# Expert stage of a graph and mixture network: 40 tiles of 384 tokens in place of 56 of 256, and down products with the weights stationary

## The reference, cut to what matters

```python
N_ROWS, D, E, H, TOP_K = 6250, 256, 8, 1024, 2
logits = xt @ Wr + br
top_p, top_idx = top_k(softmax(logits), TOP_K)
weights = top_p / top_p.sum(-1, keepdims=True)
xn = (xt - mean(xt)) * rsqrt(var(xt) + 1e-5)
xe = xn[None] * ln_g[:, None, :] + ln_b[:, None, :]
h = gelu(einsum('end,edh->enh', xe, W1) + b1[:, None, :])
y = einsum('enh,ehd->end', h, W2) + b2[:, None, :]
out = (weights[:, :, None] * y_of_the_two_chosen_experts).sum(1)
```

## Time and profile before

| | before |
|---|---|
| median of 3 runs | 7407.15 us (7395.56 to 7407.92) |
| the profiled execution's own time | 7444.26 us |
| its span, first to last instruction | 7442.4 us |
| mean granted TensorE clock | 0.717 |
| first expert transpose to last expert product | 4033.57 to 5615.09 us |
| POOL busy | 3724.7 us (50%) |
| PE busy | 3556.7 us (48%) |

### The profile page before, as it was taken

How to read it: one execution, slowest core, us unless ns; L and a number is a source line. 1 busy time by engine, 2 the same in 40 slices (tenths; PEclk the granted TensorE clock), 3 DMA queues, 4 the chain that set the end, 5 groups by cost and what they waited for, 6 DMA issues and landing times. The chain is left out here.

```text
span 7442.4 us, 64871 instructions
## 1 busy us (share of the span) xinstructions
PE 3556.7 (48%) x13693; PEld 2571.0 (35%) x13694; DVE 2821.2 (38%) x6837; ACT 831.5 (11%) x2066; POOL 3724.7 (50%) x3797
## 2 busy tenths in 40 slices
PE   3113964444433444444331222299991455555429
PEld 1001543333322333333230100178881334333317
DVE  5106854344435344344380000011114455555761
ACT  0001930000002000000130000022221100000222
POOL 4772046666662666666507766600005566666221
PEclk7556977777766777777655555599995777777759
DMA  3001023333311333332012000022214233333140
GB/s 133 1 0 37 12 59 91 92 91 90 92 41 50 90 90 91 90 92 84 1 40 92 2 4 4 9 73 79 82 56 137 86 90 90 89 90 89 56 159 18
DMA packets 290139, 497.46 MB, mean 67 GB/s; under 512 B 99253, under 2 KB 182880, under 8 KB 290048
## 3 DMA queue, kind: packets, MB, share of 16 engines
q0 software_dynamic: 163264, 345.19, 16.3%
q1 hardware_dynamic: 125696, 150.28, 6.2%
q10 hardware_dynamic: 1088, 1.05, 0.1%
HBM read 487.50 MB, written 92.89 MB: 78 GB/s over the span
## 5 line engine op out<-in xcount | busy, mean ns | idle before, releaser
L956 PE MATMUL sum_sums<-sum_got,sum_onehot 128*128 x4992 | 1583.0, 477 | 1780.9 <-DVE acc L1118 1392.7
L888 POOL DMA_INDIRECT sum_got<-xn,edge_row x1568 | 1534.1, 978 | 1175.3 <-issue 449.0
L956 PEld LDWEIGHTS sum_sums<-sum_got,sum_onehot 128*128 128x128 f32 x4992 | 1145.5, 239 | 2203.4 <-issue 2004.8
L1118 DVE TENSOR_TENSOR acc<-acc,sum_sums 128x257 f32 (+1 forms) x2496 | 1052.4, 422 | 1808.9 <-remote 1213.4
L888 POOL DMA_INDIRECT sum_got<-h,edge_row x784 | 754.0, 962 | 493.9 <-issue 223.9
L1248 POOL DMA_INDIRECT table<-rec,addr x784 | 762.4, 972 | 347.4 <-issue 305.5
L1754 PE MATMUL moe_f_ps_y<-xb,moe_f_hT 128*128 128x256 f32 x1792 | 475.8, 398 | 298.0 <-issue 297.8
L1738 PE MATMUL moe_f_ps_h<-moe_f_xT,xb 128*128 128x256 f32 x1792 | 472.1, 397 | 285.5 <-issue 285.5
L1819 DVE TENSOR_TENSOR moe_f_y<-moe_f_ps_y,moe_b 128x256 f32<-128x256 f32 x112 | 42.3, 419 | 1337.6 <-PE moe_f_ps_y L1754 650.6
L1248 POOL DMA_INDIRECT table<-sort_rec,sort_addr x392 | 404.5, 1032 | 199.3 <-issue 119.7
L1586 POOL DMA_INDIRECT moe_out_c_got<-moe_out,place_i x98 | 95.1, 971 | 815.5 <-PEq L1544 777.0
(11 more groups left out here) (481 smaller groups left out, 3420.1 us busy)
## 6 DMA issues: line engine op xcount, KB each, us to landing
xb<-in_L_ffn_W SPq DMA_DIRECT2D x112, 1024.0 KB
sum_got<-xn,edge_row POOLq DMA_INDIRECT x1568
moe_in<-acc SPq DMA_DIRECT2D x28, 512.0 KB
moe_f_xin<-moe_in SPq DMA_DIRECT2D x56, 256.0 KB
moe_out<-moe_f_y SPq DMA_DIRECT2D x56, 256.0 KB
xn<-xb SPq DMA_DIRECT2D x14, 896.0 KB
table<-rec,addr POOLq DMA_INDIRECT x784
sum_got<-h,edge_row POOLq DMA_INDIRECT x784
```

The costliest lines, as they stand in the source:

```text
L888: pool.indirect_dma_start(got[:, c % SU, 0:D], None, source, bass.IndirectOffsetOnAxis(ap=p.edge_row[:, c:c + 1], axis=0)).then_inc(s_got[ ...
L956: mm = nc.tensor.matmul(sums[k % 2][j], onehot[:, (k % QUARTERS) * HALF + j, :], flat(got[:, bass.ds(where[n % PLAN], 1), :]), start=True, ...
L1118: v.tensor_tensor(a, a, sums[k % 2][j], ALU.add).then_inc(s_added[j], 1)
```

## The change

The expert stage gets a function of its own, `moe`, with tiles of `MT` = 384 rows (`MC` = 3 blocks of 128) and `MOE_TILES` = 40. The up products move 384 columns. The down products have the 128 x 128 blocks of W2 stationary and move the 384 columns of `hT`; the result `yT` has D on partitions, so b2 becomes one number a partition (`p.moe_b2` is [128, 2, 8] and not [128, 8, 256]), the zero product goes, and the new `back` turns the result with 6 transposes, which VectorE copies to `y`. `flip` has 6 transposes. PSUM is dealt out anew: two banks `ps_f` shared by `flip` and `back`, four `ps_h`, two `ps_y`. On TensorE `flip(t+2)` now comes behind the first two ups of the tile, and `back(t-1)` behind the ups of j = 4 and 5. On SP the store of tile t-1 comes ahead of the weight loads. Four tiles are written out ahead of the loop in place of two. `Binning.starts` counts full tiles by comparing with multiples of 384. The zero fill of `moe_in` covers 15360 rows in place of 14336.

```diff
-MOE_TILES = (TOP * N + EX * (FT - 1)) // FT
+MC = 3
+MT = MC * P
+MOE_TILES = (TOP * N + EX * (MT - 1)) // MT
+MOST = -(-N // MT)
...
-        c.link(nc.vector.tensor_copy(self.total_i[:], self.total[:, 0:B + 1]))
-        c.link(nc.vector.tensor_single_scalar(self.total_i[:], self.total_i[:], shift, ALU.arith_shift_right))
-        c.link(nc.vector.tensor_copy(self.full[:], self.total_i[:]))
+        wide = [P, B + 1, MOST]
+        c.link(nc.vector.tensor_tensor(self.past[:], self.total[:, 0:B + 1].unsqueeze(2).to_broadcast(wide),
+                                       self.step[:].unsqueeze(1).to_broadcast(wide), ALU.is_gt))
+        c.link(nc.vector.tensor_reduce(self.full[:], self.past[:], AX, ALU.add))
...
+        ps_f = [p.ps(f"f_ps_f{i}", [P, 512], ctx) for i in range(2)]
+        ps_h = [p.ps(f"f_ps_h{i}", [P, 512], ctx) for i in range(4)]
+        ps_y = [p.ps(f"f_ps_y{i}", [P, 512], ctx) for i in range(KB)]
...
+            def store(t, k):
+                sp.wait_ge(s_y, 2 * t + 2)
+                sp.dma_start(at(y_dram, t), y[:, k, :, :]).then_inc(s_out[k], 16)
...
                 if left > 4:
-                    sp.wait_ge(s_flip, t + 3)
+                    sp.wait_ge(s_flip, KB * (t + 3))
                     load_x(t + 4, k)
+                if not (isinstance(t, int) and t == 0):
+                    store(t - 1, 1 - k)
+
                 gate(sp, s_down, t + 1, s_seen)
...
-                sp.wait_ge(s_y, 2 * t + 2)
-                sp.dma_start(at(y_dram, t), y[:, k, :, :]).then_inc(s_out[k], 16)
...
+                for kb in range(KB):
+                    if kb == 0:
+                        pe.wait_ge(s_x[k], 16 * uses + 16)
+                    if isinstance(t, int) and t in (1, 2, 3):
+                        pe.wait_ge(s_xT, KB * (t - 1) + kb + 1)
+                    elif not (isinstance(t, int) and t == 0):
+
+                        pe.wait_ge(s_y, 2 * t - 8 + kb + 1)
+                    for b in range(MC):
+                        last = nc.tensor.transpose(ps_f[kb][:, b * P:(b + 1) * P], xin[:, k, b, kb * P:(kb + 1) * P],
+                                                   p.ident[:])
+                    last.then_inc(s_flip, 1)
+
+            def back(t, left):
+
+                pe.wait_ge(s_yT, KB * t + KB)
+                for a in range(2):
+                    if left > 2:
+                        pe.wait_ge(s_xT, KB * (t + 3) + a + 1)
+                    else:
+                        pe.wait_ge(s_y, 2 * t - 2 + a + 1)
+                    for b in range(2 * a, min(2 * a + 2, MC)):
+                        for d in range(KB):
+                            last = nc.tensor.transpose(ps_f[a][:, (b % 2) * D + d * P:(b % 2) * D + (d + 1) * P],
+                                                       yT[:, d, b * P:(b + 1) * P], p.ident[:])
+                    last.then_inc(s_back, 1)
...
-                if j % 2 == 0 and not first:
-
-                    pe.wait_ge(s_act, HB * t - HB + j + 2)
+                if not (first and j < 4):
+
+                    pe.wait_ge(s_act, HB * t + j - 3)
...
-                    nc.tensor.matmul(ps_y[k][:].rearrange("p b d -> p (b d)"), zero[0:1, 0:P], zero, start=True, stop=False)
-                if j % 2 == 0:
-                    pe.wait_ge(s_act, HB * t + j + 2)
-                for blk in range(2):
-                    mm = nc.tensor.matmul(ps_y[k][:, blk, :], hT[:, k, j, blk * P:(blk + 1) * P], w2[:, wk, j, :],
-                                          start=False, stop=(j == HB - 1 and blk == 1))
+                    if not (isinstance(t, int) and t == 0):
+
+                        pe.wait_ge(s_yT, KB * t)
+                    pe.wait_ge(s_w2[k], 16 * uses + 16)
+                pe.wait_ge(s_act, HB * t + j + 1)
+                for d in range(KB):
+                    mm = nc.tensor.matmul(ps_y[d][:, 0:MT], w2[:, k, j, d * P:(d + 1) * P], hT[:, k, j, :],
+                                          start=(j == 0), stop=(j == HB - 1))
...
             def tile(t, k, uses, left):
-                if left > 2:
-                    flip(t + 2, k, uses + 1)
                 for j in range(0, HB, 2):
                     if left > 1:
                         for a in (j, j + 1):
                             up(t + 1, 1 - k, uses + (1 if k == 1 else 0), a)
+                    if j == 0 and left > 2:
+                        flip(t + 2, k, uses + 1)
+                    if j == 4 and not (isinstance(t, int) and t == 0):
+                        back(t - 1, left)
                     for a in (j, j + 1):
                         down(t, k, uses, a)
...
             def tile(t, k, uses, left):
                 if left > 2:
-                    evacuate(t + 2, k, uses + 1)
...
+                    enter(t + 2, k)
+                if not (isinstance(t, int) and t == 0):
+                    leave(t - 1, 1 - k, uses if k == 1 else uses - 1)
+                e = expert(dve, t)
                 dve.wait_ge(s_down, t + 1)
...
+                for d in range(KB):
+                    v.tensor_scalar(yT[:, d, :], ps_y[d][:, 0:MT], b2[:, d, bass.ds(e, 1)], None,
+                                    ALU.add).then_inc(s_yT, 1)
...
-                        (p.moe_b2[:, e, :], io["L0_ffn_b2"][e, :].partition_broadcast(P))]
+                        (p.moe_b2[:, :, e], columns(io["L0_ffn_b2"][e, :]))]
```

More of the change, by code:

```diff
@@ L1464, in _ @@
                 c.done(v.tensor_scalar(past[:], p.node_no[:], float(N), None, ALU.is_ge))
-                c.done(v.tensor_scalar(gap[:, 0:1], p.part_no[:], float(MOE_TILES * FT), None, ALU.add))
+                c.done(v.tensor_scalar(gap[:, 0:1], p.part_no[:], float(MOE_TILES * MT), None, ALU.add))
                 c.settle()
@@ L1594, in _, with moe @@
                 norm.apply_part(act, p.acc, p.xb, i, U * i, U * i + U)
-def ffn(p, source, result, count, weights, experts, func, scatters):
+def moe(p, source, result, weights, scatters):
     nc, v = p.nc, p.nc.vector
     W1, W2, b1, b2 = weights
+    count = MOE_TILES
     with ExitStack() as ctx:
[L1607 to L1623, removed]
-        s = lambda name: p.sem("f_" + name, ctx)
[L1625 to L1630, removed]
@@ L1631, in ffn @@
         block = ctx.enter_context(nc.Block())
-        pairs = (count - 4) // 2
-        rest = count - 2 - 2 * pairs
-        UPS = HB // 2
+        HEAD = 4
+        pairs = (count - HEAD - 2) // 2
+        rest = count - HEAD - 2 * pairs
         def over_tiles(eng, tile):
-            for t in range(2):
-                tile(t, t, 0, count)
+            for t in range(HEAD):
+                tile(t, t % 2, t // 2, count)
             with eng.Fori(0, pairs) as i:
                 for k in range(2):
-                    tile(2 * i + 2 + k, k, i + 1, count)
+                    tile(2 * i + HEAD + k, k, i + HEAD // 2, count)
@@ L1706, in tile @@
                     load_w2(k, *plans[0])
[L1707 to L1710 removed]
+            ahead = (count - HEAD - 4) // 2
+            for t in range(HEAD):
+                tile(t, t % 2, None, count)
             with sp.Fori(0, ahead) as i:
                 for k in range(2):
[L1713 to L1714 removed]
+                    tile(2 * i + HEAD + k, k, None, count)
+            for t in range(HEAD + 2 * ahead, count):
                 tile(t, t % 2, None, count - t)
+            store(count - 1, (count - 1) % 2)
             for k in range(2):
@@ L1775, in _ @@
             over_tiles(pe, tile)
+            back(count - 1, 0)
         @block.scalar
@@ L1804, in _, with leave @@
-            v.memset(zero, 0.0).then_inc(s_zero, 1)
-            evacuate(0, 0, 0)
-            evacuate(1, 1, 0)
+                    dve.wait_ge(s_flip, KB * t + kb + 1)
+                    v.tensor_scalar(xT[:, k, kb, :], ps_f[kb][:, 0:MT], p.ln_g[:, kb, bass.ds(e, 1)],
+                                    p.ln_b[:, kb, bass.ds(e, 1)], ALU.mult, ALU.add).then_inc(s_xT, 1)
+            def leave(t, k, uses):
+                if not (isinstance(uses, int) and uses == 0):
+                    dve.wait_ge(s_out[k], 16 * uses)
+                for a in range(2):
+                    dve.wait_ge(s_back, 2 * t + a + 1)
+                    n = min(2, MC - 2 * a)
+                    v.tensor_copy(y[:, k, 2 * a:2 * a + n, :].rearrange("p b d -> p (b d)"),
+                                  ps_f[a][:, 0:n * D]).then_inc(s_y, 1)
@@ L1817, in tile @@
-                for blk in range(2):
-                    bias = flat(b2[:, bass.ds(e, 1), :]) if experts else b2[:]
-                    v.tensor_tensor(y[:, k, blk, :], ps_y[k][:, blk, :], bias, ALU.add).then_inc(s_y, 1)
+                for d in range(KB):
+                    v.tensor_scalar(yT[:, d, :], ps_y[d][:, 0:MT], b2[:, d, bass.ds(e, 1)], None,
+                                    ALU.add).then_inc(s_yT, 1)
             over_tiles(dve, tile)
-        if scatters is not None:
-            @block.gpsimd
-            def _(pool):
-                scatter.run(pool, *scatters)
```

(4 more changed lines are left out.)

118 lines of the change are left out of this document (50 added, 68 removed).

## The result

The changed kernel takes 7434.69 us (7428.67 to 7442.68, 5 runs), the kernel before beside it 7407.15 (7395.56 to 7412.26, 5 runs): ratio 1.0040, 95% interval 1.0028 to 1.0051, so 28 us slower, with 21 and 38 us as the interval's ends. The prediction said 7435. That the two agree within 1 us is closer than either can be told.

What follows compares the result with a forecast made beforehand. TensorE was taken to bound the expert stage: 51.3 us more at full clock less 26 from the slow half gives +25.5. With tail 2.8 and head 0.3, about +28 on 7407 makes 7435 us (8 in 10: 7408 to 7465).

Steps and rivals of the forecast that it cites:

- What bounds the stage: Expert stage: TensorE sets its end in both halves, at half clock while POOL scatters and at full clock afterwards.
- 2.80 us a pair in the slow half: Expert stage while POOL scatters: each weight load and matmul pair takes 2.80 us whatever its columns; 337 pairs by 4857.5.
- 0.3225 us for 384 columns: Up and down products at full clock: a 384-column matmul takes 0.3225 us, extended from 128 and 256 columns.
- 51.3 us at full clock: Expert stage if all at full clock: 40 tiles of 21.96 us against 56 of 14.77, 51.3 us more.
- 26 us given back by the slow half: Expert stage under the scatters: pairs of 384 columns do more at the same price, 26 us off the added cost.
- Tail and head: Ends of the expert stage: +2.8 us after the last product, +0.3 us for the larger first load.
- Waits costed at nothing: Expert stage: new waits, such as down's for yT, cost 0; a few us a tile in the slow half, recovered in bursts.
- cheaper long matmuls: Rival, fast half: 384 columns cost less than 0.3225 us; halfway, at 0.269, the result is 7313 us; chance 0.03.
- earlier scatters: Rival, POOL's scatters in the expert stage: they end up to 60 us sooner, -26 us net, 7381; chance 0.09.
- DVE on the way: Rival, fast tiles: TensorE waits 1 to 2 us for yT's return trip, +36 to +72 us, 7490; chance 0.10.
- fewer pairs: Rival, slow half: late signals cost a tile's worth of pairs, 22 us, giving 7457; chance 0.05.
- no change at all: Rival, expert stage: 40 tiles cost as 56 did, 7407 us; chance 0.03.

Runs made afterwards that it cites:

- e11: Changed kernel with the expert stage's scatters writing 64 records each in place of 128, on a chip with the slow half: 7435.66 us, one run.
- e12: Kernel before with its 588 scatters in a stage ahead of the expert stage, on a chip with the slow half: 7482.93 us, ratio 1.0105.
- e1: Kernel before with its 588 scatters in a stage ahead of the expert stage, on a chip without the slow half: 6403.94 us, ratio 1.1343.
- e2: Changed kernel with its scatters in a stage ahead of the expert stage, on a chip without the slow half: 6461.9 us, ratio 1.1452.
- e5: Changed kernel as it is, run again on a chip without the slow half: 5709.21 us, ratio 1.0112 to the kernel before.
- e4: Kernel before with 60 tiles of 256 rows, the four more holding zeros: 5706.05 us, ratio 1.0110.
- e6: Changed kernel without the turn of the result (240 transposes and 80 copies left out): 5678.6 us, ratio 1.0055 to the kernel before.
- e8: Kernel before with a PSUM bank for each row block of down and no zero product in the expert stage: 5620.46 us, ratio 0.9954.
- e9: Kernel before without the zero product in both the expert stage and stage half, on a chip with the slow half: 7379.3 us, ratio 0.9963.
- e10: Kernel before, unchanged, run for a trace on a chip with the slow half: 7411.57 us.

## Why the prediction was right, point by point

- *What bounds the stage, and 2.80 us a pair in the slow half, whatever its columns*: held with 384 columns (76 pairs in 212.79 us). e11 and e12 add that it needs the scatters to be running and is the same with 64 records a scatter as with 128.
- *0.3225 us for 384 columns*: measured 0.3225. The three lengths are 0.110, 0.2159 and 0.3225: two cycles of 2.4 GHz a column and 2.5 ns. The Trainium skill (TensorE: Matmul & The Clock Gate, Back-to-back issue gap) has for a single matmul the formula N / 2.4 + 2.5 ns. With the code's 128, 256 and 384 columns for N it gives about half of what the traces show; with twice the columns it gives 109.2, 215.8 and 322.5 ns, and by that the traces agree. Its figures for sustained streams, which the prediction weighed, they do not bear out for float32.
- *51.3 us at full clock, +2.8 and +0.3*: sum 54.4. On chips without the slow half the stages grew by 55.1 (e1 and e2) and 54.7 (e5). In parts, by the stages: additional rows +59.4 for 59 (e4), turn 26.9 for 28 (e6), zero products 838.9 - 810.6 = 28.3 for 28.6 (e8); by the medians of whole kernels 60.4, 30.6 and 27.5.
- *26 us given back by the slow half*: 339 pairs for 337; 782.8 us left for 781.2. Between the chips it is 54.7 - 27.8 = 27. That is shown by the count of pairs and by this comparison of chips, and by no pair of kernels on one chip.
- *Tail and head*: +2.55 for 2.8 at the end, where the prediction's own terms add up to 2.9. The head was not measured by itself.
- *Waits costed at nothing*: none in a full tile. In the slow half I said a few us a tile for yT, and it is 50: the term was mis-sized because ACT's lateness of 42 us stood in for DVE's 88. The reason that it costs nothing, the burst, held for twenty pairs as for six. It was luck, though, that the last of these waits ended at 4512.21 + 212.8, that is at 4725, well ahead of the last scatter at 4811; e9 shows what one costs that outlasts the scatters, and here it could have been up to 18 pairs of 0.3225 us, 6 us by estimate.
- *Rivals*: cheaper long matmuls are out by the tile of 21.95, earlier scatters by 806.8 us, DVE on the way by rows without a wait, fewer pairs by 339, and no change at all by the interval, which begins at 21 us. The premise against earlier scatters, that TensorE presses on POOL, is not borne out: alone they take 796 us on D.
- *The profiled execution's 37 us above the median, carried over as no part of the difference*: the changed kernel's execution does not lie above its median, so the 7472 of the sum did not come; the choice to add the difference to the median was right. On D the kernel before had a profiled execution of 7411.57 us, next to its median of 7406.44.

One thing that the prediction took for granted does not hold: that the kernel has a slow half. On chips B and C it has none, and there the same change costs 61 us on 5648, 1.1%.

## What to carry to other kernels

Price a new tile size by rows of the matmul's own dtype at two lengths, and then ask how many rows of padding the size adds: here the longer tile took fewer instructions at the same rate a column, and the 1024 rows of zeros were the cost. A stage that hides beside another engine's work must be read twice, as each half has its own price; what pays in one (fewer, longer matmuls) may pay nothing in the other. Where two accumulations share a PSUM bank and a zero product clears it, one bank for each makes the zero product unnecessary: 27 us here.

## What the runs showed of the hardware

- The same kernel takes 7407 us on chips A and D and 5646 on B and C. By the traces of e10 (D) and e8 (C) 870 of the 1761 us lie ahead of the expert stage (first transposes at 4013.9 and 3143.6) and 146 behind it (7409.7 - 5599.75 against 5618.4 - 3954.2); the stage itself has 1586 on D and, by e8's 810.6 and its 27.5, 838 on C. The other stages were not taken apart.
- On A and D TensorE gets through one pair in 2.80 us while scatters run, at 128, 256 or 384 columns, at 64 or 128 records a scatter, and with 1.27 or a mean of 1.40 us between scatters. After a wait of 50 us it runs 20 to 21 pairs in 9 to 12 us, just those that the pace would have brought in the meantime. DVE and ACT come late: 88 us (DVE) and 42 us (ACT) after the product that they wait for. That reads as instructions that arrive at 1.40 us each and are kept while the engine waits, so that the engine itself is not slowed. It is a reading of the counts; what delivers them so slowly, and why on these chips alone, was not tried and stays open.
- Scatters alone, on D, begin at 1.28 us each and end at 1.40, with TensorE, VectorE and ScalarE idle. Beside TensorE their mean is 1.40 as well, from 4200 to 4800 in e10 (429 scatters), with 64 records too (e11, 430). So the two engines share this pace, and neither seems to set it for the other.
